# Two transposes ahead of a context value tile, and one dense tile ahead of two output tiles

## The reference

```
x = x + L0_xattn(layernorm(x), ctx, ctx, mask, Wq, Wk, Wv, Wo)   # 32 query heads, 8 key heads, size 128, rotary, 30*tanh(l/30), masked softmax
x = x + L0_ffn(layernorm(x), A, B, Wr)                           # 4 low-rank experts of rank 16, the top 2 mixed
x = x + L1_xattn(layernorm(x), ctx, Wq, Wk, Wv, Wo)              # 16 query heads, 4 key heads, size 96; keys and values from [ctx, layernorm(x)]
x = x + L1_ffn(layernorm(x), W, bias, A, Bf, coeffs, scales)     # x W^T + bias + 16 low-rank updates
```

## Time and profile before

| what | value |
|---|---|
| median of three runs | 854.36 us (853.88 to 854.86) |
| the profiled execution | 854.5 us |
| its span, first to last instruction | 852.7 us |
| PE busy | 839.6 us, 98% |
| PEld busy | 700.2 us, 82% |
| DVE busy | 490.3 us, 57% |
| ACT busy | 353.0 us, 41% |
| POOL busy | 310.7 us, 36% |
| granted clock of TensorE | 1.000 |

### The profile page before, as it was taken

The page is one execution under the profiler, slowest core; times in us unless marked ns, Lnnn a source line. Parts: engine busy times, 40 slices in busy tenths (PEclk is TensorE's granted clock), DMA queues, the critical chain, the costliest instruction groups (busy, mean ns, idle before and its releaser), DMA issues.

```text
span 852.7 us, 12369 instructions
## 1 busy us (share of the span) xinstructions
PE 839.6 (98%) x4758; PEld 700.2 (82%) x4758; DVE 490.3 (57%) x869; ACT 353.0 (41%) x827; POOL 310.7 (36%) x239
## 2 busy tenths in 40 slices
PE   6999999999999999999999999999999999999998
PEld 5878888888888888888877788888988888888776
DVE  6856655655555655555566536465344445455783
ACT  6443123123123123123123242667776766676642
POOL 4777534634534634534536330112010210211222
PEclk9999999999999999999999999999999999999999
DMA  8112211311211311311211122101010110310002
GB/s 302 50 64 75 86 38 41 109 38 38 87 38 39 111 38 38 87 38 40 85 38 52 46 78 81 26 26 50 13 38 13 54 47 1 107 43 1 1 1 100
DMA packets 24891, 48.15 MB, mean 56 GB/s; under 512 B 3584, under 2 KB 4736, under 8 KB 24704
## 3 DMA queue, kind: packets, MB, share of 16 engines
q1 hardware_dynamic: 24400, 47.22, 18.2%
q10 hardware_dynamic: 432, 0.14, 0.1%
HBM read 45.12 MB, written 2.23 MB: 56 GB/s over the span
## 4 chain that ended last, share of the span: by engine, by line
PE 93%; DVE 2%; POOL 2%; ACT 1%; DMA 1%; issue 1%; SPq 0%; POOLq 0%; DVEq 0%
PE PB L1161 22%; PE PB L1163 22%; PE PB L1162 22%; PE PB L1320 8%; PE PB L1251 4%; PE PB L1335 3%; PE PB L1225 3%; PE PB L1352 3%; PE PB L1168 3%; PE PB L1235 1%; PE PB L1272 1%; DMA xs<-in_x 1%; PE PB L1374 1%; POOL qb L730 1%; ACT Eb L809 1%
## 5 line engine op out<-in xcount | busy, mean ns | idle before, releaser
L945 DVE TENSOR_TENSOR xs<-xs,PB 128x512 f32<-128x512 f32 x112 | 76.8, 686 | 120.3 <-PE PB L1163 113.1
L730 POOL TENSOR_TENSOR qb<-qb,arena 128x512 f32<-128x512 f32 x64 | 83.7, 1308 | 151.3 <-DVE arena L1023 151.3
L781 ACT ACTIVATE Oh<-PB 128x512 fp32r<-128x512 f32 (+2 forms) x160 | 69.2, 467 | 82.7 <-PE PB L1352 44.9
L1161 PE MATMUL PB<-WOh,Oh 128*128 128x512 f32 x248 | 96.6, 390 | 0.0
L1163 PE MATMUL PB<-WOh,Ol 128*128 128x512 f32 x248 | 96.5, 389 | 0.0
L1162 PE MATMUL PB<-WOl,Oh 128*128 128x512 f32 x248 | 96.5, 389 | 0.0
L1020 DVE TENSOR_TENSOR qb<-PB,ropeq 128x512 f32<-128x512 f32 x64 | 44.2, 691 | 69.4 <-PE PB L1163 68.3
L707 POOL TENSOR_TENSOR WQl<-stage,WQh 128x512 fp32r<-128x512 f32 x38 | 49.0, 1292 | 91.4 <-ACT WQh L781 90.1
L1161 PE MATMUL PB<-xTh,WQh 128*128 128x512 f32 x192 | 76.5, 399 | 0.0
L1163 PE MATMUL PB<-xTh,WQl 128*128 128x512 f32 x192 | 74.8, 390 | 0.0
L1162 PE MATMUL PB<-xTl,WQh 128*128 128x512 f32 x192 | 74.7, 389 | 0.0
(11 more groups left out here) (212 smaller groups left out, 2080.5 us busy)
## 6 DMA issues: line engine op xcount, KB each, us to landing
stage<-in_wq SPq DMA_DIRECT2D x44, 256.0 KB, 2.9
stage<-in_wo SPq DMA_DIRECT2D x44, 256.0 KB, 2.6
arena<-recs SPq DMA_DIRECT2D x32, 256.0 KB, 3.9
stage<-in_wk SPq DMA_DIRECT2D x13, 256.0 KB, 2.6
arena<-in_ctxT SPq DMA_DIRECT2D x8, 256.0 KB, 4.4
stage<-in_wv SPq DMA_DIRECT2D x8, 256.0 KB, 3.8
xs<-in_x SPq DMA_DIRECT2D x8, 256.0 KB, 5.7
out<-xs SPq DMA_DIRECT2D x8, 256.0 KB, 2.0
```

What stands on the lines that cost most here:

```text
L730: e.tensor_tensor(dst, dst, tmp, ALU.add).then_inc(s_radd)
L781: return e.activation(dst, src, ACT.Copy)
L945: e.tensor_tensor(xs[:, i, :], xs[:, i, :], PB[b][:, :], ALU.add).then_inc(free[b])
L1161: e.matmul(dst, Ah, Bh, start=(k == 0), stop=False)
```

## The change

In the first place (phase 2, tiles 0 to 3) the transposes of tiles 0 and 1 are done together ahead of the value tile `v1` 0,6, their `xn` successors and splits likewise, and `mgT` 1 goes behind the transposes of tile 2. In the second place the first dense tile goes ahead of the output tiles `e1` 30 and 31, and `e1` 30 no longer stands between the transposes of tiles 1 and 2. No operation is added or taken away, and banks are dealt out anew by the ring.

```diff
     gates(1)
     v1(0, 5)
     ring[0:0] = [2]
-    for i in range(4):
+    for i in range(2):
         stage("xT", 2, i)
-        if i < 2:
-            step("xn", 2, i + 2)
+    for i in range(2):
+        step("xn", 2, i + 2)
+    for i in range(2):
         step("xsplit", 2, i)
-        if i == 1:
+    v1(0, 6)
+    for i in range(2, 4):
+        stage("xT", 2, i)
+        step("xsplit", 2, i)
+        if i == 2:
             stage("mgT", 1)
-        if i in (0, 3):
-            v1(0, 6 + i // 3)
+    v1(0, 7)
...
         step("xsplit", 3, i)
-        if i == 1:
-            stage("e1", 30)
-            step("stats", 3, 6)
     for i in LO:
         step("add_bias", i)
+    stage("dense", 0)
+    stage("e1", 30)
+    step("stats", 3, 6)
     stage("e1", 31)
     step("stats", 3, 7)
     step("rstd", 3, 4)
-    for i in range(3):
+    for i in range(1, 3):
         stage("dense", i)
```

## The result

The changed kernel takes 858.33 us (median of five, 856.9 to 859.1) against 854.36: ratio 1.0043, 95% interval 1.0028 to 1.0058. The forecast was 855.9 in a range from 854.7 to 857.7; the time lies 0.6 above the range. The profiled execution took 858.33 us, its span is 856.5 and its mean granted clock 0.995, where before it was 1.000.

A forecast was written before the change was run, and what follows sets the result against it. The prediction took TensorE, busy for 839.6 of 852.7 us, to bound the kernel. Its terms, -1.0 + 2.4 + 0.1 = +1.5 us, gave 855.9 us from the median of 854.36, in a range from 854.7 to 857.7.

The forecast's parts named there:

- Place 1: x tiles of the second norm: a 1.40 us wait goes and a new one of 0.39 comes, -1.0 us.
- Place 2: x tiles of the last norm: waits of 1.37, 0.92 and 1.94 us replace one of 1.86, +2.4 us.
- Transposes 4 and 5: Last norm, behind `e1` 30 and 31: transposes 4 hidden by 0.2 us, those of tile 5 wait, +0.1 us.
- Half clock after place 2: Last norm: TensorE falls to the clock's lower level, 1.2 GHz, costing 1.7 us, time 857.6 us; chance 0.17.
- the first sign of being wrong: Last norm: matmuls of the dense tile 0.43 us apart in the profile after would show the forecast wrong.
- The other two rivals: Second norm's change gives nothing, 856.9 us, chance 0.08; last norm's dense 0 is free of `xTl` 0, 853.9, chance 0.10.

## Why the prediction was wrong, step by step

- Place 1, -1.0 us: right. 1.07 in the profile, 0.74 between medians, with its new wait of 0.36 (0.39 said) and the deltas not held.
- Place 2, +2.4 us of waits: right. 1.37, 0.91 and 1.89 against 1.37, 0.92 and 1.94. Without the half clock the changed kernel takes 855.7, shown by filling the waits, where the forecast said 855.9.
- Transposes 4 and 5, +0.1: right. Those of tile 5 come 0.07 late (838.57 - 837.71 = 0.86 against 0.79).
- The step that failed: the sum has no term for the clock. It takes dense 0 at full clock, 2.72 us, and it measured 5.15. The clock was left to the first rival, "Half clock after place 2", at a chance of 0.17, and by the clock of 0.995 to 0.998 it happened in all five runs of the changed kernel and all five of the second place alone. The low chance was argued from the stretch of 2.7 us that left the clock at its level, the nearest row, to one of 5.9 us, twice as long, with PE at work for 1.6 us of it. That step the rows did not carry, and the runs show another outcome: none of the profiles with the old second place has the fall there, two waits within 3.9 to 4.0 us go with a clock of 0.998 in 2, 4 and 2 of eleven runs, three waits within 5.8 us in all ten. Matmuls of the dense tile 0.43 us apart are the first sign of being wrong that the prediction names.
- The rival's own size was off too: 1.7 us said, 2.43 in the profile. So even the range, drawn to end just past the rival as it was sized, ends below the measured time. The price was counted over the 3.56 us that the slow matmuls at the start take. The half clock lasted from 821.2 to 828.0 and covered all of dense 0: twelve matmuls at 0.43 in place of 0.23 are 2.4. In the profile of the second place alone it was shorter (eight matmuls, 1.6), which is what was priced. With the size mended the rival says 855.7 + 2.4 = 858.1; measured 858.3.
- The rival came true for another reason than the one offered, that transposes do not count: with 33 more transposes in the waits PE did nothing else for 5.8 us, and the clock stayed.
- The other two rivals did not happen: the first place keeps its gain alone, and dense 0 was held by `xTl` 0, since moving two statistics behind it took the wait away.

## What to carry to other kernels

When an edit puts several short waits of TensorE one behind another, look at them with the short work between as one stretch, and price half clock over the whole tile that follows beside the waits themselves. Here the added waiting cost 2.31 us and the half clock 2.43. A tile moved forward is free only if what it reads is ready in the order of the producing engine: two statistics of 0.9 us each on DVE, needed by nobody yet, made most of the third wait. Look on the producing engine first: swapping the head copies and two activations on ACT took 0.79 us of waiting away, where moving tiles on PE lost 4.5.

## What was not expected of the hardware

- Float32 transposes at 0.11 us each kept the granted clock at 2.4 GHz for 5.8 us (855.78, clock 1.000 in eleven runs); 16 transposes with three waits in the same time did not.
- The fall needs no single long wait. In the changed kernel's profile the longest idle time before it was 1.37 us by starts; 4.0 us after the last output matmul the level was already changing. In the profile of the second place alone it changed only after 5.9 us.
- The half clock's length differs between executions, 6.8 us in the changed kernel's profile and about 3.4 in those of the second place alone and of the last wait filled. The changed kernel's times spread over 2.2 us, against 0.98 for before in its first five runs. A part of any spread comes before both places: the profiled executions come to the first transposes of the second norm between 567.28 and 568.91 us.
- A wait of TensorE for DVE can be shown as "issue": the 1.66 us before dense 0 end with `xTl` 0.
